# A relational graph layer on one Trainium2 core: the next block's key chain, hit products and hit cast at later tiles, and the own-row load issued by ScalarE

## The reference, cut to what matters

```python
# x: 6250 x 256, src/dst/edge_type: 206250 (sorted by dst), edge_weight1: 206250 x 1, weight: 16 x 256 x 256
transformed = jnp.einsum('ni,rio->rno', h, weight)
msg = transformed[rel_type, src] * norm
out = jax.ops.segment_sum(msg, dst, num_segments=h.shape[0])
x = _layernorm(x + out, axis=-1)
```

## Time and profile before

| | |
|---|---|
| three runs | 2549.6, 2565.3 and 2580.5 us |
| the profiled execution | 2584.9 us, of which 2583.2 are the span |
| TensorE busy | 2219.3 us, 86% of the span |
| GpSimd busy | 1560.6 us, 60% |
| VectorE busy | 1151.6 us, 45% |
| ScalarE busy | 271.2 us, 10% |
| mean granted TensorE clock | 0.926 of full |

### The profile page before, as it was taken

How to read it: one execution, slowest core, us unless ns; L and a number is a source line. 1 busy time by engine, 2 the same in 40 slices (tenths; PEclk the granted TensorE clock), 3 DMA queues, 4 the chain that set the end, 5 groups by cost and what they waited for, 6 DMA issues and landing times.

```text
span 2583.2 us, 33166 instructions
## 1 busy us (share of the span) xinstructions
PE 2219.3 (86%) x12267; PEld 1956.2 (76%) x12267; DVE 1151.6 (45%) x2871; ACT 271.2 (10%) x559; POOL 1560.6 (60%) x1675
## 2 busy tenths in 40 slices
PE   5589889889988998888888888888898888888888
PEld 4477777778777777777777778777787777777777
DVE  4344444344444443544444345444544444444443
ACT  2011101101111010101110011011101100110100
POOL 5666666656665666666666566666666666666660
PEclk8799999989998999999989998998999999999998
DMA  4333333333333333333333333333333333333331
GB/s 134 101 94 95 94 94 93 94 90 90 93 95 90 94 93 93 94 92 94 93 99 92 91 91 97 91 91 95 96 94 93 96 90 93 93 94 94 89 92 17
DMA packets 107084, 238.86 MB, mean 92 GB/s; under 512 B 30580, under 2 KB 54176, under 8 KB 106926
## 3 DMA queue, kind: packets, MB, share of 16 engines
q0 software_dynamic: 79056, 215.91, 29.5%
q1 hardware_dynamic: 27870, 20.81, 2.8%
HBM read 230.13 MB, written 6.62 MB: 92 GB/s over the span
## 4 chain that ended last, share of the span: by engine, by line
PE 77%; another core or an unknown queue 8%; issue 7%; DVE 4%; ACT 2%; SPq 0%; DMA 0%; DVEq 0%
PE ps_a L799 55%; PE ps_z L766 14%; PE ps_z L768 7%; DVE a_lo L581 2%; ACT a_hi L678 2%; DVE spread L605 1%; DMA w_raw<-in_L_gnn_weight 0%; PE ps_m L750 0%; SPq L344 0%; ACT meta L666 0%; PE ps_m L736 0%; DVE key L533 0%; DVE key_hit L542 0%; DVE hits L545 0%
## 5 line engine op out<-in xcount | busy, mean ns | idle before, releaser
L433 POOL DMA_INDIRECT rows<-in_x,idx x1646 | 1557.0, 946 | 958.5 <-issue 441.4
L799 PE MATMUL ps_a<-spread,rows 128*128 128x128 f32 (+15 forms) x8820 | 1817.3, 339 | 305.4 <-issue 174.3
L799 PEld LDWEIGHTS ps_a<-spread,rows 128*128 128x128 f32 x8820 | 1394.0, 201 | 481.4 <-issue 219.2
L766 PE MATMUL ps_z<-w_parts,a_hi 128*128 128x512 f32 x1568 | 875.3, 560 | 29.8 <-DVE a_lo L581 25.0
L605 DVE TENSOR_SCALAR spread<-ps_i,key,meta 128x272 f32<-128x272 f32 (+13 forms) x1715 | 750.7, 502 | 50.4 <-remote 29.7
L581 DVE TENSOR_TENSOR a_lo<-ps_a,a_hi 128x512 fp32r<-128x512 f32 x392 | 252.4, 686 | 1055.3 <-ACT a_hi L678 990.7
L768 PE MATMUL ps_z<-w_parts,a_lo 128*128 128x256 f32 x1568 | 453.9, 289 | 7.7 <-issue 7.7
L678 ACT ACTIVATE a_hi<-ps_a 128x512 fp32r<-128x512 f32 x392 | 212.8, 595 | 1848.9 <-PE ps_a L799 1483.5
L766 PEld LDWEIGHTS ps_z<-w_parts,a_hi 128*128 128x128 f32 x1568 | 317.1, 202 | 64.8 <-DVE a_lo L581 28.0
L768 PEld LDWEIGHTS ps_z<-w_parts,a_lo 128*128 128x128 f32 x1568 | 316.8, 202 | 37.6 <-issue 13.5
L528 DVE CAST idx<-meta 128x35 int32<-128x35 f32 x50 | 10.4, 208 | 120.7 <-ACT meta L666 117.2
(11 more groups left out here) (52 smaller groups left out, 132.0 us busy)
## 6 DMA issues: line engine op xcount, KB each, us to landing
rows<-in_x,idx POOLq DMA_INDIRECT x1646
xr<-in_x SPq DMA_DIRECT2D x48, 128.0 KB
out<-z_out SPq DMA_DIRECT2D x48, 128.0 KB
w_raw<-in_L_gnn_weight SPq DMA_DIRECT2D x16, 256.0 KB
raw<-in_src SPq DMA_DIRECT2D x48, 17.5 KB
raw<-in_dst SPq DMA_DIRECT2D x48, 17.5 KB
raw<-in_edge_type SPq DMA_DIRECT2D x48, 17.5 KB
raw<-in_edge_weight SPq DMA_DIRECT2D x48, 17.5 KB
```

The lines of the kernel that those rows point to most:

```text
L433: pool.indirect_dma_start(rows[:, rows_slot(b, t), :], None, x, bass.IndirectOffsetOnAxis(ap=idx[:, b % 2, t:t + 1], axis=0)).then_inc(row ...
L766: pe.matmul(zk, a_hi[:, ak, h, r, :], w_parts[:, r, h, :, :].rearrange("p a f -> p (a f)"), start=n == 0, stop=False, skip_group_check=True)
L799: ins = pe.matmul(ps_a[:, g % OPEN, h, (begin - g * GN) * R:(stop - g * GN) * R], rows[:, rows_slot(b, t), h * P:(h + 1) * P], spread[:, s ...
```

## The change

Three steps of the preparation move to later tiles, for all blocks but block 0, whose tiles are written out and stay as they were: the key chain from tile 6 to 16, the hit products from 8 to 20 and the hit cast from 12 to 31. And the load of the own rows leaves SyncE, where it stood behind the store; ScalarE issues it at its tile 20, after a wait for the sum that reads the buffer last (`residual_added`). The first block's load stays on SyncE.

```diff
--- before.py
+++ after.py
@@ -106,8 +106,8 @@
 
 
 
-    PREPARE = (1, 2, 4, 6, 8, 12)
-    PREPARE_0 = tuple(t + 19 for t in PREPARE)
+    PREPARE = (1, 2, 4, 16, 20, 31)
+    PREPARE_0 = (20, 21, 23, 25, 27, 31)
     SEEK_ROW, SEEK_GATHER, SEEK_EDGE, SEEK_TURN, SEEK_TABLE = 2, 5, 10, 11, 13
     WEIGHTS_AT = {2 * n + 1: n for n in range(R)}
     WEIGHTS_BEFORE = 7
@@ -115,6 +115,7 @@
     CONFIRM = 3
     PRODUCT_FROM = 4
     NORM_AT = 10
+    OWN_AT = 20
 
     products_after = []
     done_products = 0
@@ -388,7 +389,6 @@
 
                 sp.wait_ge(rows_normalised, b)
                 sp.dma_start(out[(b - 1) * SB:b * SB, :], z_out[:, :]).then_inc(rows_out, 16)
-                sp.dma_start(xr[:, :], x[b * SB:b * SB + SB, :]).then_inc(own_rows_in, 16)
             for b in range(NB - 3, NB):
                 if b == NB - 3:
 
@@ -401,9 +401,7 @@
                     load_edges(TAIL, tails)
 
                 sp.wait_ge(rows_normalised, b)
-                rows_of = min(SB, N - b * SB)
                 sp.dma_start(out[(b - 1) * SB:b * SB, :], z_out[:, :]).then_inc(rows_out, 16)
-                sp.dma_start(xr[0:rows_of, :], x[b * SB:b * SB + rows_of, :]).then_inc(own_rows_in, 16)
 
             sp.wait_ge(rows_normalised, NB)
             sp.dma_start(out[(NB - 1) * SB:N, :], z_out[0:LAST, :]).then_inc(rows_out, 16)
@@ -705,6 +703,12 @@
                         wait(act, variance_steps, b, 2, -2)
                         act.activation(z_std[:, :], z_mv[:, 1:2], ACT.Sqrt, bias=eps_col[:, :]).then_inc(
                             deviation_made, 1)
+                    if rows_ and t == OWN_AT and b <= NB:
+
+                        wait(act, residual_added, b, 1, -1)
+                        rows_of = min(SB, N - (b - 1) * SB)
+                        act.dma_start(xr[0:rows_of, :], x[(b - 1) * SB:(b - 1) * SB + rows_of, :]).then_inc(
+                            own_rows_in, 16)
 
             convert_edges(0)
             copy_edges(0)
```

## The result

| | before | changed |
|---|---|---|
| median, us (runs) | 2567.7 (4) | 2837.1 (4) |
| lowest to highest | 2549.6 to 2580.5 | 2826.0 to 2851.6 |
| profiled execution | 2584.9 | 2831.3 |
| mean granted clock | 0.926 | 0.873 |

The changed kernel took 1.106 times the time of before, 95% interval 1.097 to 1.115: 270 us slower, where 195 had been forecast. The experiments then showed a limit that these runs alone could not show: the loss belongs to a setting, of the chip or of the way it was run, in which both kernels were timed here, and it is absent in another, where both take 2100 us.

The account below looks back on a forecast made before the run. It took TensorE, starved by GpSimd's long unbroken gather runs, as the bound at 51.3 us a block. 41.2 + 8.5 + 3.5 + 2.3 = 55.5 us, 4.2 more in 47 blocks, gave 2760 us; range 2430 to 2960.

Parts of the forecast that it names:

- the theory of starvation: TensorE nearly stops beyond some 12 us of unbroken GpSimd gathers and comes free 2 us after the last.
- ideal pass of 41.2 us: One block of TensorE's tiles at full clock, against 51.3 us taken: 10.1 us lost in each block.
- GpSimd idle and behind by 22 tiles: Block start: GpSimd waits for the later keys some 8 us, then leads TensorE by 22 tiles instead of 30.
- The first run is 15 gathers: GpSimd at block start: two ring checks pass, the one before gather 15 more often fails; the run takes 18.45 us.
- rival 2: The third ring check passes, so the first run is 20 gathers: 489 us more, 3050 us; chance 0.12.
- 8.5 us lost and 3.5 of half clock behind it: TensorE's loss a block from the first run of 15 gathers, 8.5 us, plus 3.5 us at half clock after it.
- The second run, ten gathers, loses 2.3: Gathers 15 to 24 of a block, 14.3 us with the release, cost TensorE 2.3 us.
- At tiles 5 to 12 it is idle and costs nothing.: GpSimd, idle while TensorE does tiles 5 to 12, was to cost TensorE no time there.
- Hit steps and own rows at 0: Moving the hit product and cast, and the own-row load to ScalarE, was each to change the time by 0.
- Nothing replaces the waits: Rival: VectorE's waits at tiles 6 and 12 go, and TensorE's waits for spreads with them: 2365 us; chance 0.20.
- A wash: Rival: GpSimd's idle stretch shields tiles 5 to 12, balancing the longer run: 51.3 us a block, 2565 us; chance 0.12.
- Partly: Rival: the first run is short by luck of the phase in most blocks: 2600 to 2645 us; chance 0.18.

Follow-up runs that it names:

- the late start alone: Kernel before, with only GpSimd held before its first gather of a block until TensorE has summed tile 11 of the block before: 2903.72 us, 1.124.
- the stops: Changed kernel, with GpSimd waiting before gathers 8, 16 and 24 until the gather before has landed: 1.023 in setting A, 1.128 in setting B.
- the keys at 13: Changed kernel, with the key chain at tile 13 in place of 16: 2637.57 us, 1.023.

## Why the prediction was right, and where it was not

**The block of before and the theory of starvation.** Right for the setting in which it was read. The ideal pass of 41.2 us is near what setting B shows: (2045.4 - 5.2)/49 = 41.6 us by the key chain's first cast in the changed kernel, 42.0 from block 3 on. That is no test of the 41.2, which is TensorE's pace, since GpSimd's own gathers need 1646 x 1.25/49 = 42.0 us a block. Of the missing 10.1 us of a block, 9.2 are that setting's loss (51.25 - 42.01, from the end of block 2 to the end of block 48). Three runs bear out that the length of GpSimd's runs is what costs in A: the late start alone brings the loss without the new order, the stops take it away with the new order in place, and with the keys at 13 it moves to earlier tiles. One reading of before was wrong in size: the longest unbroken run was not the 25 of the earlier trace rows but block 0's, 36 gathers from 6 to 52.8 us (35 and the start-up's). It bears the theory out. From 34 to 50 us TensorE is busy 3.62 of 16 us:

```profile
34.00:50.00 16.00, 3.62 (x9) 2.58 (x9) 3.82 (x10) 0.63 (x1) 12.35 (x13) 0.61 0.52 141
```

**Key chain behind the lower part of group 0, GpSimd idle and behind by 22 tiles.** Right. The forecast was 6 to 12 us of wait; it is 479.7/49 = 9.8 us, and the 47 runs of 15 start with TensorE in tile 12 (38 blocks) or 11 (nine), where 12 or 13 were forecast.

**The first run is 15 gathers.** Right, in every block from the third on, 47 of them. The third ring check, called close, failed each time, so the run of 20 (rival 2) never came.

**8.5 us lost and 3.5 of half clock behind it.** Right in mechanism, too large in size. Tiles 23 to 26 take 15.3 us against 5.9 in setting B: 9.4 instead of 12.0. TensorE kept its pace for 13.3 us in the run shown and not 12, and did a few matmuls after that.

**The second run, ten gathers, loses 2.3.** Too large as well. At the end of it stands tile 32 with 2.0 us instead of 1.0: about 1 us.

**"At tiles 5 to 12 it is idle and costs nothing."** This step failed. GpSimd is idle there, but tile 7 takes 4.3 us instead of 1.2, and tiles 5 to 13 take 15.5 against 11.4: 4.1 us a block. That is less than the 7.2 that they lost before (18.6), but not nothing. They are the tail of the run of eight or nine just before. TensorE has gaps until 1190.53, 3.6 us after the last gather was issued, and the eight matmuls that start there still go at half clock (0.72 over the window of 6 us shown above):

```profile
1186.71 0.36 PE L772 MATMUL ps_z<-w_parts,a_lo 128*128 128x256 f32 x1 [0.38 <-issue]
1187.40 0.28 PE L803 MATMUL ps_a<-spread,rows 128*128 128x144 f32 x1 [0.34 <-issue]
...
1189.55 0.54 PE L803 MATMUL ps_a<-spread,rows 128*128 128x144 f32 x3 [0.71 <-issue]
...
1190.53 1.91 PE L803 MATMUL ps_a<-spread,rows 128*128 128x80 f32 x8
```

The run of eight follows the ten after a pause of 2.4 us only. I had counted each run from zero; two runs with a short pause between them may act as more than either. The stops in A speak for and against it: all pauses inside a block are 2.1 us there and most of the loss stands behind the last run, but tiles 23 to 26, behind the first such pause, lose next to nothing (6.0 us against 5.9), and tiles 27 to 34, behind the second, little (9.4 against 9.1). It was not tried by itself, and why this run costs anything is open.

**The sum.** Forecast 55.5 us a block from 41.2 + 14.3. Measured, by the rows of the changed kernel in the table: 41.9 us in B and 56.3 in A, so 14.4 lost, of which tiles 23 to 26 have 9.4, tiles 5 to 13 have 4.1 and tiles 27 to 34 have 1.1, with 0.2 the other way. Two terms too large and one missing nearly cancel, so that the closeness of the sum is in part luck. The growth is 4.87 us a block by TensorE's timeline over blocks 3 to 48 (56.12 - 51.25), 224 us in these 46, where 4.2 x 47 = 197 was forecast. Another 22 us come in blocks 0 to 2, which end at 226.5 us instead of 204.5. The forecast had nothing there, and it is not shown to be the change's: block 0, whose steps are unchanged, ends between 77.4 and 91.3 us in the seven profiled executions in A. The difference of the two profiled executions is 246.4. In the medians it is 270.

**Hit steps and own rows at 0.** The own rows, right. The hit steps were not 0: alone they gain 1.4%, 2574.4 - 2542.0 = 32 us of the 106.1 they remove. Moved together with the key chain they can't be told apart from it.

**The rivals.** "Nothing replaces the waits" (2365) is refuted in A: both waits went and TensorE lost more. Its argument, that both waits are the largest that TensorE sees, misread the rows: they are VectorE's, and TensorE's largest was the 174.3 us with no semaphore behind them. In B it is also wrong, for another reason: there is nothing to gain. "A wash" was the result in B, but not by its mechanism, a shielded stretch; in B there is no stall to shield. It was given for a program whose block takes 51.3 us and says nothing of one that takes 41.6. "Partly" did not occur: the phase was the same in all blocks.

**What the prediction did not name** is the widest of the uncertainties, that the stall is no property of the program. Every number in it was read in setting A, and it holds there.

## What to carry to other kernels

Look at how long the gathering engine runs without a pause, and at what stands just behind such a run on TensorE, before you move a step that releases it. A step that leaves the critical path can still be the one that paces another engine. Removing a wait here turned a wait spread over the block (30 tiles of lead, runs of five and ten) into one long idle stretch and a burst of 15. And before tuning against a stall with no semaphore behind it, time the kernel before several times, apart, and on more than one chip: where it takes 2100 us in one place and 2570 in another, an order tuned against the stall may be worth nothing in the other, and pauses put in to cure it cost 13% there.

## What the runs showed of the hardware that was not expected

**Two settings, 22% apart.** The kernel before took 2549.6 to 2618.9 us in the runs of A and 2097.4 to 2102.2 in 50 runs of B, with nothing between. The records of the experiments give a number for the chip: 7 and 3 in A, 10 and 3 in B, number 3 within minutes. If one number is one chip, the setting can change on a chip; whether it is the same chip, the records do not say.

**What differs, by the traces.** Not GpSimd: a gather takes 946 to 949 ns at the median in both and they follow each other after 1.25 us. Not the transfers: the gathers' packets took 29.5% of 2583.2 us in A (the kernel before) and 36.3% of 2098.7 in B (the changed one), 762 us both times. What differs is when TensorE's work and its increments get through beside the gathers. ScalarE's wait for the turned columns, which rests on TensorE's increment, shows it. It is 251.9 us in 42 waits, at most 7.3, for the changed kernel in A, and in B:

```profile
ACT meta L664 <- PE ps_m L754: 29.3, 50, 1.0
PE ps_a L803 <- DMA rows<-in_x,idx: 26.9, 47, 1.6
```

The releaser differs too: "remote" in A, that is one whose event could not be matched, and TensorE's transpose in B. The page's line of the gathers ends with a landing time of 2.8 us in B and has none in A, where most landings have no event of their own in the trace: 9,063 landing events for the changed kernel in A, 29,785 for the same kernel in B. Other engines' events are missing in A too: of VectorE's 1715 spreads 1290 have one there, of TensorE's 1715 tiles 1636, and in B all but one. TensorE's transposes of the edge columns have theirs in both settings, and show the delay: the increment comes 5.8 us after the last transpose's end at the median in the changed kernel in A, 3.2 us in the kernel before, and 0.014 us in B. VectorE's spreads and ScalarE's rounded parts, where an event is there, have it after 0.01 us in A as in B.

So in A events are lost or merged, and TensorE's increments are late. This points at the path by which increments and TensorE's instructions move, and not at the data. It is a reading of where the traces differ and was not tested; whether the bytes, the descriptors or the completions of the gathers load that path is open, since the runs made for it met setting B. Nor is the recording itself ruled out: events are missing in A, every timed execution of both settings comes with a recorded span and clock, and no run without them is there to compare.

The Trainium skill, "TensorE: Matmul & The Clock Gate", section "The cost: per-tile semaphore tail", puts the cost of one matmul's increment at about 26 ns. In B the increment of the turned columns comes 0.014 us after the transpose, which leaves room for that figure; in A it comes 5.8 us after it at the median, and there the measurement decides against it.

The Trainium skill, "Perfetto Trace Analysis", section "DMA Instruction — SWDGE (GPSIMD)", has the end of such an instruction in a profile as the end of making descriptors and not of moving data. The traces agree: half the bytes left the 946 ns at 944 and 945 ns and moved the landing from 2.8 to 2.5 us.
